# Three stages of a fused four-layer kernel in another order

## The reference, cut to what matters

```python
# layer 0: five steps of a stencil in x and y, with D, c0, E, cm_*, cp_* computed from the input
for _ in range(K):                      # K = 5
    prev = h
    h = D * (c0 * h0 - 2.0 * E * h + cm_x * jnp.roll(h, 1, axis=2) + cp_x * jnp.roll(h, -1, axis=2)
             + cm_y * jnp.roll(h, 1, axis=3) + cp_y * jnp.roll(h, -1, axis=3))
    h = h + D * (2.0 * DT) * fsrc       # fsrc is the normalized input, and also the first h
    h0 = prev
# layer 1: a 3x3 convolution of 64 channels with bias
# layer 2: layer norm, a selective scan block, skip, layer norm, a 64x64 projection
xs = silu(causal_conv(x @ in_proj))     # z is the other half of in_proj
delta = softplus(dt @ dt_proj_w.T + dt_proj_b)
h = exp(delta * A) * h + (delta * u) * B ;  y = sum_n h * C      # 1024 steps, 16 states
y = (y + u * D) * silu(z)
# layer 3: a two-dimensional DCT
```

## Time and profile before

| | us |
|---|---|
| median of 3 runs | 911.88 |
| lowest and highest | 911.01, 912.39 |
| the profiled execution | 911.18 |
| its span, first to last instruction | 909.2 |
| PE busy | 734.8 (81%) |
| DVE busy | 802.6 (88%) |
| ACT busy | 560.2 (62%) |
| POOL busy | 527.1 (58%) |

### The profile page before, as it was taken

How to read it: one execution, slowest core, us unless ns; L and a number is a source line. 1 busy time by engine, 2 the same in 40 slices (tenths; PEclk the granted TensorE clock), 3 DMA queues, 4 the chain that set the end, 5 groups by cost and what they waited for, 6 DMA issues and landing times.

```text
span 909.2 us, 10555 instructions
## 1 busy us (share of the span) xinstructions
PE 734.8 (81%) x3866; PEld 499.9 (55%) x3866; DVE 802.6 (88%) x682; ACT 560.2 (62%) x960; POOL 527.1 (58%) x243
## 2 busy tenths in 40 slices
PE   3895999877667788788799889988766677888896
PEld 2342344344466777678655434435446566787783
DVE  6979997769999998999969899775999999989984
ACT  2962242227849898979486723313585987897942
POOL 3105899020479698778510479911127978878851
PEclk9999899999799899999989899999989999999999
DMA  3002000000445455455200120000033455545431
GB/s 113 1 24 69 0 1 0 0 1 0 140 151 174 142 190 191 139 186 179 77 1 0 59 58 0 0 1 0 1 98 120 148 177 173 201 153 182 160 110 23
DMA packets 34065, 78.18 MB, mean 86 GB/s; under 512 B 15704, under 2 KB 15840, under 8 KB 34016
## 3 DMA queue, kind: packets, MB, share of 16 engines
q1 hardware_dynamic: 32608, 76.23, 25.1%
q0 software_dynamic: 320, 1.05, 0.5%
q10 hardware_dynamic: 1088, 0.26, 0.1%
HBM read 70.71 MB, written 2.62 MB: 81 GB/s over the span
## 4 chain that ended last, share of the span: by engine, by line
DVE 35%; PE 29%; ACT 16%; issue 16%; POOL 2%; DMA 0%; DVEq 0%; POOLq 0%; SPq 0%; ACTq 0%
ACT arena L957 13%; PE ps L748 7%; DVE arena L1773 7%; PE ps L509 6%; DVE ps L1764 6%; PE ps L548 4%; DVE HS L1773 3%; DVE arena L1728 3%; PE ps L762 2%; PE ps L640 1%; ACT ps L957 1%; PE ps L662 1%; DVE arena L1748 1%; DVE arena L1667 1%; DVE arena L1646 1%
## 5 line engine op out<-in xcount | busy, mean ns | idle before, releaser
L396 POOL TENSOR_TENSOR arena<-arena 128x1024 f32<-128x1024 f32 x85 | 200.5, 2368 | 59.8 <-DVE arena L1773 54.6
L957 ACT ACTIVATE arena<-arena 128x128 f32<-128x128 f32 (+3 forms) x412 | 157.0, 455 | 86.9 <-DVE arena L1667 67.7
L1773 DVE TENSOR_TENSOR_SCAN arena<-arena,ps 128x1024 f32<-128x1024 f32 x86 | 194.6, 2276 | 9.7 <-ACT arena L957 5.5
L957 ACT ACTIVATE arena<-arena,Amat 128x1024 f32<-128x1024 f32 x128 | 143.0, 1141 | 7.2 <-DVE arena L1773 6.0
L640 PE MATMUL ps<-mat,arena 128*128 128x128 f32 x1016 | 136.6, 279 | 5.6 <-POOL arena L396 5.2
L599 PE MATMUL ps<-mat,arena 128*128 128x128 f32 x560 | 81.6, 294 | 64.4 <-DVE arena L1773 36.9
L640 PEld LDWEIGHTS ps<-mat,arena 128*128 128x128 f32 x1016 | 118.4, 145 | 9.8 <-POOL arena L396 7.9
L748 PE MATMUL ps<-arena,mat 128*128 128x512 f32 x240 | 110.9, 615 | 14.4 <-DVE arena L1643 14.4
L396 POOL TENSOR_TENSOR arena<-HS,arena 128x1024 f32<-128x1024 f32 x42 | 100.1, 2382 | 29.7 <-DVE HS L1773 27.0
L599 PEld LDWEIGHTS ps<-mat,arena 128*128 128x128 f32 x560 | 65.8, 146 | 79.4 <-DVE arena L1773 46.8
L957 ACT ACTIVATE arena<-ps 128x1024 f32<-128x1024 f32 (+2 forms) x55 | 46.1, 849 | 87.2 <-PE ps L486 45.4
(11 more groups left out here) (219 smaller groups left out, 1340.3 us busy)
## 6 DMA issues: line engine op xcount, KB each, us to landing
arena<-c_rows SPq DMA_DIRECT2D x128, 512.0 KB, 3.8
arena<-arena SPq DMA_DIRECT2D x16, 252.0 KB
out<-arena SPq DMA_DIRECT2D x28, 64.0 KB, 2.3
xres<-x POOLq DMA_DIRECT2D x4, 256.0 KB, 5.2
xres<-x SPq DMA_DIRECT2D x4, 256.0 KB, 4.1
convw<-conv_w SPq DMA_DIRECT2D x1, 576.0 KB
c_rows<-ROWS SPq DMA_DIRECT2D x4, 128.0 KB, 1.9
mat<-mats SPq DMA_DIRECT2D x1, 448.0 KB, 3.5
```

The source lines that it names most:

```text
L396: tt(HC[s % 2], HS[s % 3], CB[s % 4], ALU.mult).then_inc(S("hc"), 1)
L957: return nc.scalar.activation(out_, in_, func, bias=bias, scale=scale, accum_out=accum_out)
L1773: nc.vector.tensor_tensor_scan(HS[s % 3], DA[s % 3], PS[q][:, :], 0.0, ALU.mult, ALU.add).then_inc(S("scan"), 1)
```

## The change: what it does

No arithmetic is added or left out. Calls move in the lists of four engines, four waits move, two buffers are exchanged, and one row of 14 small matmuls is added per half. The core of the diff:

```diff
-        for name, at in [("SQ", "W3"), ("XN", "R1"), ("V1", "W2"), ("X3", "W4"), ("T1", "W3"), ("A2", "W2"),
+        for name, at in [("SQ", "W3"), ("XN", "R1"), ("V1", "W2"), ("T1", "W3"), ("A2", "W2"),
+        F[1]["X3"] = A[1]["sden"]
-        HS = [D[0]["W4"], D[0]["W5"], sb("HS2", L)[:, :]]
+        HS = [D[0]["W4"], sb("HS2", L)[:, :], D[0]["W5"]]
...
             def first_two_sources(h):                        # POOL
-                pool.wait_ge(S("a0_G"), 2 * h + 2)
+                pool.wait_ge(S("a_Pm"), 2 * h + 1)
...
                 source(h, 0)
+                pool.wait_ge(S("a_Pm"), 2 * h + 2)
                 with pool.Fori(0, STEPS) as t:
                         pool.wait_ge(S("a_Q6"), 2 * h + k + 1)
-                        pool.wait_ge(S("a_Pm"), 2 * h + k + 1)
...
+                pool.wait_ge(S("dbu"), len(Z_STEPS) * h + 2)
                 relu_part(h, 1)
                 relu_part(h, 2)
...
                 group_mean(D[0], h, 1, 0)                    # PE
+                spin(PS[1], 14)
                 wino_product(h, 0, 0)
...
+                xn_channels(h, 0)
                 group_mean(D[1], h, 2, 1)
-                spin(PS[1], 4)
-                xn_channels(h, 0)
+                x_in_proj(h, 0, 0)
                 n2_pixels(h, 1)
-                x_in_proj(h, 0, 0)
                 z_in_proj(h, 0, 0)
                 x_in_proj(h, 0, 1)
+                dt_proj(h, 0, 0)
                 xn_channels(h, 1)
-                dt_proj(h, 0, 0)
...
                 turn_first_rows(h)
+                z_in_proj(h, 1, 1)
                 pe.wait_ge(S("b_kept"), h + 1)
                 b_rows(h, 0)
                 b_rows(h, 1)
-                z_in_proj(h, 1, 1)
                 dt_proj(h, 1, 1)
...
                     copy_x3(h - 1, 1)                        # ACT, second half
-                    from_D(h, 0)
                     reciprocal(h, 1)
                     small_group_shift(D[1], h - 1, 3, 1)
                     scale(h - 1, 1)
+                    from_D(h, 0)
                     relu(h, 1, 1)
                     copy_a2(h - 1, 1)
-                    copy_out(h - 1, 1)
...
                     first_seed(h, k)
                     if h > 0 and k == 0:
+                        copy_out(h - 1, 1)
                         from_D(h, 1)
...
                 square(h, 0, 0)                              # ACT, norms
+                layer_scale(h, 0)
                 norm2(h, 1)
-                layer_scale(h, 0)
...
                 exp_of(h, 2)
+                silu_x(h, 1, 1)
                 keep_rows(h, 0)
+                silu_z(h, 1, 1)
                 ln_of(h, 0)
+                keep_first_b(h)
                 ln_of(h, 1)
-                keep_first_b(h)
                 ln_of(h, 2)
-                silu_x(h, 1, 1)
-                silu_z(h, 1, 1)
                 decay(h, 0)
...
-                stt(img(a["Sc"]), img(a["Dc"]), 2 * DT, frm(a["fz"])[:, 1:33, 1:33], ALU.mult, ALU.mult)   # DVE, last_source
+                stt(img(a["Sc"]), img(a["Dc"]), 2 * DT, img(PS[3]), ALU.mult, ALU.mult)
...
-                if h > 0 and k == 1:                         # y_neighbours
-                    dve.wait_ge(S("final"), 2 * h)
...
+                if h > 0 and k == 1 and t == 0:              # products, ahead of the write of sden
+                    dve.wait_ge(S("final"), 2 * h)
...
+                dve.wait_ge(S("a1_act"), 3 * STEPS * h + 2)  # last_first_sources
-                tt(img(a["g"]), img(a["X"]), frm(a["fz"])[:, 1:33, 1:33], ALU.mult).then_inc(S("a1_g"), 1)
+                tt(img(a["g"]), img(a["X"]), img(PS[3]), ALU.mult).then_inc(S("a1_g"), 1)
...
                     x_neighbours(h, 0)                       # DVE, second half
+                    minus_E(h, 0)
                     fractions_D(h, 1)
-                    minus_E(h, 0)
                     times_D(h, 1, 0)
                     fractions_K(h, 1)
                     y_neighbours(h, 1)
+                    times_D(h, 1, 1)
+                    x_neighbours(h, 1)
                     products(h, 0, 0)
                     minus_E(h, 1)
-                    times_D(h, 1, 1)
                     last_first_sources(h)
-                    x_neighbours(h, 1)
                     products(h, 1, 0)
...
                 add_conv(h, 1)                               # DVE, norms
+                normalize(0, h, 0)
                 stats(D[1]["X2"], D[1], h, 2, 1)
-                normalize(0, h, 0)
                 group_norm(D[1], h, 2, 1)
-                causal(h, 0, 0, rest=False)
+                causal(h, 0, 0, range(4))
                 variance(1, h, 0)
-                causal(h, 0, 0, first=False)
+                causal(h, 0, 1, range(2))
                 normalize(1, h, 0)
-                causal(h, 0, 1)
-                causal(h, 1, 0)
+                causal(h, 0, 1, range(2, 4))
                 relu_x(h, 0, 0)
+                causal(h, 1, 0, range(4))
                 relu_x(h, 0, 1)
-                causal(h, 1, 1)
+                causal(h, 1, 1, range(4))
                 one_plus(h, 0)
+                relu_x(h, 1, 0)
                 one_plus(h, 1)
                 first_relu_part(h)
-                relu_x(h, 1, 0)
                 one_plus(h, 2)
                 delta(h, 0)
                 first_delta_u(h)
-                delta(h, 1)
                 scan_input(h, 0)
-                delta(h, 2)
                 scan_input(h, 1)
                 scan_step(h, 0)
                 scan_step(h, 1)
+                delta(h, 1)
                 relu_x(h, 1, 1)
                 scan_input(h, 2)
                 scan_step(h, 2)
+                delta(h, 2)
                 one_plus(h, 3)
```

More of the change, by code:

```diff
@@ L1315, in _ @@
                 silu_x(h, 0, 0)
+                abs_x(h, 0, 0)
                 layer_scale(h, 1)
-                abs_x(h, 0, 0)
                 silu_x(h, 0, 1)
@@ L1611, in last_source @@
                 dve.wait_ge(S("a_D"), 2 * h + 2)
-                stt(img(a["Sc"]), img(a["Dc"]), 2 * DT, frm(a["fz"])[:, 1:33, 1:33], ALU.mult, ALU.mult).then_inc(S("a_Sc1"), 1)
+                stt(img(a["Sc"]), img(a["Dc"]), 2 * DT, img(PS[3]), ALU.mult, ALU.mult).then_inc(S("a_Sc1"), 1)
             def y_neighbours(h, k):
                 a = A[k]
-                if h > 0 and k == 1:
-                    dve.wait_ge(S("final"), 2 * h)
                 dve.wait_ge(S("a_K"), 2 * h + k + 1)
@@ L1716, in x2_norm, with causal @@
                 group_norm(D[k], h, 2, k)
-            def causal(h, k, b, first=True, rest=True):
+            def causal(h, k, b, some):
                 d, i = D[k], 2 * h + b
-                dve.wait_ge(S(f"xi{k}"), i + 1)
-                if b == 1:
-                    dve.wait_ge(S(f"xs{k}"), i)
                 w = [vecs[:, V_CONVW + t:V_CONVW + t + 1] for t in range(4)]
-                if first:
-                    ts(d["XI"], x_ps(k, b)[:, :], w[3], None, ALU.mult).then_inc(S(f"cconv{k}"), 1)
-                for t in range(1, 4) if rest else []:
-                    dve.wait_ge(S(f"cconv{k}"), 4 * i + t)
-                    stt(d["XI"][:, t:L], x_ps(k, b)[:, 0:L - t], w[3 - t], d["XI"][:, t:L], ALU.mult, ALU.add)\
-                        .then_inc(S(f"cconv{k}"), 1)
+                for t in some:
+                    if t == 0:
+                        dve.wait_ge(S(f"xi{k}"), i + 1)
+                        if b == 1:
+                            dve.wait_ge(S(f"xs{k}"), i)
+                        ts(d["XI"], x_ps(k, b)[:, :], w[3], None, ALU.mult).then_inc(S(f"cconv{k}"), 1)
+                    else:
+                        dve.wait_ge(S(f"cconv{k}"), 4 * i + t)
+                        stt(d["XI"][:, t:L], x_ps(k, b)[:, 0:L - t], w[3 - t], d["XI"][:, t:L], ALU.mult, ALU.add)\
+                            .then_inc(S(f"cconv{k}"), 1)
             def relu_x(h, k, b):
```

## The result

The changed kernel takes 907.51 us (median of five, 904.82 to 909.09) against 912.39 us of the kernel before on the same chip: a ratio of 0.9942, with a 95% interval of 0.9920 to 0.9964. Measured once more (e12), it is 907.27 against 912.24 us, ratio 0.9937 (0.9923 to 0.9950). So it is 5 us faster, where 905.7 us, 6.2 us less than 911.9, was forecast. The profiled execution of the first measurement is the slowest of its five: 909.09 us, span 907.3. So the gain read from its trace, 1.9 us, is smaller than the gain by the times.

What follows compares the result with a forecast made beforehand. DVE (88% busy) bounds the scans, PE and nearly full GpSimd the stencil's last steps, ACT's chain the scan start. 911.18 - 7.3 - 4.9 + 2 x 3.0 = 905.0, plus 0.7 for the median: 905.7 us, range 898.0 to 911.0.

Steps and rivals of the forecast that it cites:

- Stencil, first half: Start of the first half's stencil: GpSimd's later waits and PSUM operands bring new_h earlier, gain 7.3 us.
- (a) to (c): First half's stencil: L1627 at 1.2 us, products at 82.6, field of pair 1 at 86.8, new_h at 93.7.
- the turns: SBUF-only DVE and GpSimd instructions wait for each other; at scan start L1738 and L1740 stretch to 2.9 and 3.3 us.
- Stencil, second half: Second half's stencil: new_h 5.6 us earlier, then GpSimd takes over from PE at the end; gain 4.9 us.
- Spins: 14 added matmuls before the convolution keep PE at the higher clock, winning 1.7 us per half, 0 if not.
- Norms: normalize(0) right behind the convolution: ACT's silu of image 2 starts 3.1 us earlier, the added matmuls' 1.7 included.
- Start of the scan: ACT's chain and deltas between scans: first scan 2.5 us earlier, fourth 5.2 later after it; loss 3.0 per half.
- Rival 1: Start of the scan costs nothing net, DVE runs on after ACT's early silu: 898.7 us, chance 0.18.
- rival 2: Stencil gains little, the roll DMA comes no earlier and the field stays at 88.84: 909.6 us, chance 0.13.
- Rival 3: Scan start: all four SBUF-only instructions wait for a whole GpSimd instruction, loss 7.7 per half: 915.1, chance 0.05.

Runs made afterwards that it cites:

- e12: The whole change measured once more against the kernel before: 907.27 against 912.24 us, ratio 0.9937.
- e1: Kernel before with only the stencil part of the change (GpSimd's later waits, PSUM operands, order, X3's place): 11.0 us faster than the kernel before.
- e10: Kernel before with only GpSimd's later stencil waits (first source, ahead of loop, in loop): -0.7 us gain, interval -2.2 to 0.7.
- e6: Stencil part of the change alone, but GpSimd's waits as in the kernel before: 0.2 us faster than the kernel before.
- e3: Whole change without its last stage: stencil, 14 matmuls and norms changed, start of the scan as before: 14.7 us faster than the kernel before.
- e11: Stencil, matmuls, late deltas, spread one_plus(3), ACT's logarithms first, z_in_proj(1,1) ahead of B rows; norms as before: 17.4 us faster than the kernel before.
- e2: Kernel before with the stencil part and the 14 added matmuls ahead of the convolution: 15.5 us faster than the kernel before.
- e4: Whole change, but delta(1) and delta(2) ahead of the first scans, relu_parts without the dbu wait, HS as before: 11.7 us faster than the kernel before.
- e5: Whole change, but ACT and PE at the start of the scan as before (logarithms, then silus): 7.2 us faster than the kernel before.

## Why the prediction was right

- **Stencil, first half, 7.3 us.** 6.9 in the profiled execution, 6.4 in e1. The steps (a) to (c) came as listed: L1627 1.22 us, products at 82.95 for a predicted 82.6, the field at 87.06 for 86.8, `new_h` at 94.10 for 93.7. The waits alone win 5.6 of it (e10), and without them nothing is won (e6, stencil 1 at 151.8): the turns are what was won.
- **Stencil, second half, 4.9 us.** 4.8 in the profiled execution, 5.4 in e1. The mechanism named for the end (GpSimd takes over from PE) did not show in the changed kernel, where PE was 0.3 us later; in e3 and e11 it is GpSimd. The two are level, so the number hardly depends on which ends last. e1 gains 11.0 us by the times for a predicted 12.2.
- **Spins, 1.7 a half.** 1.7 at the matmuls themselves; e2 has 4.5 +/- 2 for both halves.
- **Norms.** 3.1 us earlier at the silu of image 2 with the spins: 3.0 in e3. That it would reach the first scan was wrong. In the changed kernel the silu comes only 1.7 and 0.6 us earlier, as the matmuls of `x_in_proj(1, 0)` took 3.32 and 3.71 us. Where they ran at full clock, in e3, `bc_proj(0)` took 5.32 us instead of 3.62, and ACT waited for PE. This step failed: the term is 1.4 a half in the prediction, and it was 0.3 to 0.4 at the fourth scan of e3 and nothing that the times show.
- **Start of the scan, a loss of 3.0 a half, bounds 1.0 to 5.3.** 4.5 and 5.2 in the profiled execution, 5.7 and 1.8 in e12, a mean of 4.3. By the times the rest of the change, the spins within it, costs 5.5 (e1 11.0, the change 5.3 and 5.7) where 6.0 was forecast. The 5.2 us from the first to the fourth scan were 6.1 and 6.5: the turns came as counted (L1742 2.84 and L1744 3.26 for 2.9 and 3.3), and `relu_x(1, 1)` waited 1.2 and 1.6 us, not 0.4. The first scan came 2.0 and 0.9 us earlier, not 2.5. ACT's idle time in front of `silu_z(1, 1)` was 2.78 us for about 3.
- **The sum.** It is closer than its terms. By the traces the loss at the start of the scan is 4.3 a half, 1.3 more than forecast, about as much as the norms' missing 1.4. By the times it is not: against e3, which has the matmuls and the norms, the order of the start of the scan costs 9 us, 4.6 +/- 1.2 a half, where the prediction priced it at 6.1 (3.1 won ahead of it, 3.0 lost in all). So one term was too dear and another did not come, and that they make up for each other is luck.
- **Rival 1** (898.7) and **rival 2** (909.6, as the field would come late) are out: the field came at 87.06, and e4 and e5 each lose. **Rival 3**, all four SBUF-only instructions waiting, did not occur: two did.

The Trainium skill (SBUF — State Buffer, section "SBUF: two separate sides") states that the port pair which DVE and GpSimd share is held for a whole instruction and "the other fully blocks". The rows of e6 agree: 3.2 us instead of 1.2 for DVE's instructions, and 3.2 instead of 2.2 for GpSimd's. There both engines had work queued and alternated, so three instructions in a row paid three times.
